# Projection of a deformable convolution: three f32r products from split values, or one fp32 product from a ring of twelve rows

## What is computed

```
yp = iy + ky + offset_y;  xp = ix + kx + offset_x          # per pixel, group and tap
val = gather(y0,x0)*(1-wy)*(1-wx) + gather(y0,x0+1)*(1-wy)*wx
    + gather(y0+1,x0)*wy*(1-wx)   + gather(y0+1,x0+1)*wy*wx
val = val * sigmoid(mask)
out = einsum('bhwkc,kcf->bhwf', val, dcn_w) + dcn_b        # the projection: 9*256 products per output
return x + relu(out) + fine_cal                            # all float32
```

## Time and profile before

| | before |
|---|---|
| median of three runs | 3750.42 us (3750.3 to 3751.57) |
| profiled execution | 3750.21 us, span 3748.5 us |
| busy TensorE / weight loads | 3383.5 us (90%) / 3082.7 us (82%) |
| busy VectorE / ScalarE / GpSimd | 2643.4 (71%) / 1636.7 (44%) / 1300.2 us (35%) |
| granted TensorE clock, mean | 0.956 of 2.4 GHz |
| costliest group | L1420, 8172 records, 1269.5 us |

### The profile page before, as it was taken

How to read it: one execution, slowest core, us unless ns; L and a number is a source line. 1 busy time by engine, 2 the same in 40 slices (tenths; PEclk the granted TensorE clock), 3 DMA queues, 4 the chain that set the end, 5 groups by cost and what they waited for, 6 DMA issues and landing times.

```text
span 3748.5 us, 103646 instructions
## 1 busy us (share of the span) xinstructions
PE 3383.5 (90%) x39276; PEld 3082.7 (82%) x39276; DVE 2643.4 (71%) x4029; ACT 1636.7 (44%) x3018; POOL 1300.2 (35%) x1358
## 2 busy tenths in 40 slices
PE   8979999999999947998888998998899898988998
PEld 7869999999999936888787887887788787877888
DVE  3446666666666548878876887886887887688882
ACT  0021211211221215656654665664666665566663
POOL 1000000000000025645645555554654655455451
PEclk9989999999999978999998999998999998999998
DMA  4232232222223221111112111112111112111110
GB/s 160 78 122 42 48 72 42 48 53 39 51 51 43 32 49 30 29 32 31 31 32 32 32 33 29 31 34 32 29 33 31 30 34 36 25 33 32 31 27 23
DMA packets 352248, 159.43 MB, mean 43 GB/s; under 512 B 228724, under 2 KB 346884, under 8 KB 351620
## 3 DMA queue, kind: packets, MB, share of 16 engines
q1 hardware_dynamic: 325456, 109.56, 17.4%
q10 hardware_dynamic: 21724, 26.37, 2.1%
q0 software_dynamic: 4608, 16.78, 1.2%
HBM read 104.60 MB, written 55.23 MB: 43 GB/s over the span
## 4 chain that ended last, share of the span: by engine, by line
PE 44%; issue 7%; ACT 6%; DVE 2%; POOL 2%; ACTq 1%; DMA 1%; SPq 1%; POOLq 0%; DVEq 0%
PE eb L1420 25%; PE tb L981 9%; PE vb L1003 9%; ACT wtT L986 4%; ACT ot L1025 1%; ACT res L1012 1%; DVE wt L975 1%; PE tb L911 1%; DMA win<-cpad 1%; ACTq L1316 1%; PE vb L1018 1%; ACT val L1289 1%; ACTq L882 0%; DVE val L1362 0%; SPq L1083 0%
## 5 line engine op out<-in xcount | busy, mean ns | idle before, releaser
L1420 PE MATMUL eb<-val,wd 128*128 128x256 f32 (+2 forms) x8172 | 1269.5, 300 | 9.5 <-POOL gate L1212 8.5
L1420 PEld LDWEIGHTS eb<-val,wd 128*128 128x128 f32 x8172 | 1080.6, 199 | 44.8 <-issue 35.4
L975 DVE TENSOR_TENSOR wt<-taps_all 128x576 f32<-128x576 f32 x1024 | 938.6, 984 | 52.5 <-PE tb L981 44.6
L981 PE MATMUL tb<-ident,wt 128*128 128x128 f32 x4608 | 715.9, 282 | 63.8 <-ACT wtT L986 45.3
L986 ACT COPY wtT<-tb 128x512 f32<-128x512 f32 x1152 | 651.8, 593 | 164.8 <-PE tb L981 126.0
L1362 DVE TENSOR_TENSOR val<-vb,val 128x432 fp32r<-128x432 f32 (+1 forms) x768 | 382.6, 552 | 411.0 <-ACT val L1289 409.2
L981 PEld LDWEIGHTS tb<-ident,wt 128*128 128x128 f32 x4608 | 504.7, 141 | 185.5 <-ACT wtT L986 103.6
L1289 ACT CAST val<-vb 128x432 fp32r<-128x432 f32 (+1 forms) x768 | 342.1, 524 | 706.4 <-PE vb L1003 706.2
L480 PE MATMUL conv<-fine,wf 128*108 128x256 f32 x4608 | 591.1, 289 | 7.6 <-DVE omT L751 7.6
L480 PEld LDWEIGHTS conv<-fine,wf 128*108 128x108 f32 x4608 | 570.5, 173 | 23.0 <-issue 23.0
L1003 PE MATMUL vb<-wtT,win 64*32 64x144 f32 x16384 | 350.2, 309 | 184.3 <-issue 93.3
(11 more groups left out here) (138 smaller groups left out, 3175.7 us busy)
## 6 DMA issues: line engine op xcount, KB each, us to landing
win<-cpad SPq DMA_DIRECT2D x304, 64.0 KB
om_s<-om_d SPq DMA_DIRECT2D x1152, 12.0 KB
chunk<-in_x SPq DMA_DIRECT2D x32, 512.0 KB, 5.9
xchunk<-in_x SPq DMA_DIRECT2D x32, 512.0 KB, 4.2
r_d<-r POOLq DMA_DIRECT2D x32, 512.0 KB, 3.2
rt<-r_d SPq DMA_DIRECT2D x63, 256.0 KB, 2.9
out<-ot ACTq DMA_DIRECT2D x63, 256.0 KB, 2.2
om_d<-omT SPq DMA_DIRECT2D x64, 216.0 KB
```

What stands on the lines that cost most here:

```text
L975: return nc.vector.tensor_tensor(wt[:, g * NK:(g + 1) * NK, WQ * u:WQ * (u + 1)].rearrange("p k (a b) -> p k a b", a=WIN), of_group(0).uns ...
L981: last = nc.tensor.transpose(tb[b][:, 128 * j:128 * j + 128], wt[:, 4 * i + j, :], ident[:])
L1420: done = nc.tensor.matmul(eb[fo][:, W * r0:W * r1], wd[wp][:, half, k, 128 * fo:128 * fo + 128], source[:, at:at + r1 - r0, cols], start=f ...
```

## The change

What it does:

- The projection is one fp32 product: 36 matmuls of 256 columns a strip, from one tensor val and one tensor wd. The split of the weights (`first_parts`, `second_parts`) and of the values (L1362) is gone; `keep_values` on ScalarE is the only copy.
- val has twelve rows a tap: each parity has two rows above and four of its own, so no read wraps. The two rows above are copies of the other parity's last two, made by SP with two DMAs a strip (`duplicate_rows`, taps 0 to 5).
- wt and wtT are two tiles each, one for each hx. A half is transposed in its slot, and sampled in the next slot, after batches 1 and 4; the projection is dealt out evenly, two matmuls behind each batch, half of a strip's in slot (t, 1) and half in (t+1, 0).
- Both fo lie in one bank eb, one bank for each parity; the result is turned into it too.
- Positions and coef are computed by VectorE (`locate`), distances stay on GpSimd. Groups are ordered so that window weights take six instructions of 768 elements instead of eight of 576.
- base_y and ctr_y hold one image's 16 strips. The general path is changed alike and isn't taken here.

The core of the diff:

```diff
-        wd = [sb(f"wd{q}", [128, CH, NK, C], f32r) for q in range(2)]
+        wd = sb("wd", [128, CH, NK, C])
...
-        wt = sb("wt", [128, GH * NK, 2 * WQ])
-        wtT = sb("wtT", [128, GH * NK, 128])
+        wt = [sb(f"wt{i}", [128, GH * NK, 2 * WQ]) for i in range(2)]
+        wtT = [sb(f"wtT{i}", [128, GH * NK, 128]) for i in range(2)]
...
-        VROWS, VCOLS = 9, W + 2
+        VROWS, VCOLS = 12, W + 2
+        val = sb("val", [128, CH, NK, VROWS, VCOLS])
...
+                def duplicate_rows(s, p):
...
+                    w(sp, "ready", opened)
+                    w(sp, "projected", read)
+                    dst, src = 6 * p, 6 * (1 - p) + 4
+                    for half in range(CH):
+                        sp.dma_start(val[:, half, 0:6, dst:dst + 2], val[:, half, 0:6, src:src + 2]
+                                     ).then_inc(sems["duplicated"], 16)
...
+                    if known(s - 2, 0, ST):
+                        load_rest(s - 2)
                     if known(s + 3, 0, ST):
                         w(sp, "batched", batch_no(s, 0, NT) + 1)
                         load_offsets(sp, s + 3, True, sems["om_loaded"])
...
+                    if known(s, 1, ST):
+                        duplicate_rows(s, p)
...
+                        side(t - 1, 1 - p, 1)
+                        open_strip(t - 1, 1 - p, crossing if p == 1 else None)
+                        measure(t + 1, 1 - p, 1)
+                        side(t, p, 0)
+                        add_rest(t - 2)
+                        measure(t + 2, p, 0)
...
+                def slot(t, p, hx):
...
+                    if hx == 1 and owed:
+                        w(act, "projected", t - 1)
+                        w(act, "turned", t - 2)
+                        for fo in range(CH):
+                            finish(fo, p, m).then_inc(sems["finished"], 1)
                     for i in range(NT):
...
+                            copy_batch("act", hx, i, bank_no(t, p, hx, i)).then_inc(sems["tb_out"], 1)
+                        if i == FIRST_RUNS_AT:
+                            keep_values(*half_before(t, p, hx), 0)
+                        if i == FIRST_RUNS_AT + 1:
+                            keep_values(*half_before(t, p, hx), 1)
+                        if i == THIRD_RUN_AT:
+                            keep_values(*half_before(t, p, hx), 2)
+                        if hx == 0 and i == 5:
+                            taps(t + 1, 1 - p, 0)
...
+                    if hx == 0:
+                        if known(t + 2, 0, ST):
+                            keep(t + 2, batch_no(t, 0, NT), bank_no(t, p, 0, NT))
+                        taps(t + 1, 1 - p, 1)
...
+                def slot(t, p, hx):
+                    products(*half_after(t, p, hx))
+                    if hx == 0:
+                        cap(t + 1, 1 - p, 0)
                     else:
+                        cap(t + 1, 1 - p, 1)
+                        locate(t + 2, p)
...
+                todo = [(dy, half, dx, fo) for dy in (2, 1, 0) for half in range(CH) for dx in range(3) for fo in range(CH)]
+                EACH = len(todo) // 2
+                SHARE = EACH // NT
...
+                        done = nc.tensor.matmul(eb[q][:, 256 * fo:256 * fo + rows], wd[:, half, k, 128 * fo:128 * fo + 128],
+                                                val[:, half, k, at:at + rows // W, dx:dx + W],
+                                                start=(n == 0), stop=(n == len(todo) - 1))
...
+                def slot(t, p, hx):
+                    n = 2 * t + hx
+                    target, q, first = (t - 1, 1 - p, 0) if hx else (t - 2, p, EACH)
                     for i in range(NT):
...
+                            transpose_batch(hx, i, bank_no(t, p, hx, i)).then_inc(sems["batched"], 1)
+                        if i == FIRST_RUNS_AT:
+                            first_runs(*half_before(t, p, hx))
+                        if i == THIRD_RUN_AT:
+                            third_run(*half_before(t, p, hx))
+                        if known(target, 0, ST + 1):
+                            if first == 0 and i == 0:
+                                w(pe, "ready", target + 1)
+                                w(pe, "ob_out", target - 1)
+                            last = project(target, q, range(first + SHARE * i, first + SHARE * (i + 1)))
...
+                        if hx == 1 and i == 6 and known(t - 2, 0, ST + 1):
+                            m = W if isinstance(t, int) and t - 2 == ST else 256
+                            w(pe, "summed", t - 1)
+                            turn_result(p, m).then_inc(sems["turned"], 1)
```

More of the change, by code:

```diff
@@ L1180, in side @@
                             else:
-                                dst, src = v[:, :, east, rows, W + 1], v[:, :, west, rows, W]
-                            g.tensor_copy(dst, src.bitcast(f32)).then_inc(sems["sides"], 1)
+                                dst, src = val[:, half, east, rows, W + 1], val[:, half, west, rows, W]
+                            last = g.tensor_copy(dst, src)
+                        last.then_inc(sems["sides"], 1)
                 def open_strip(s, p, crossing):
+                    above, under = slice(0, 3), slice(6, 9)
@@ L1186, in open_strip @@
+                    if known(s, 1, ST + 1):
+                        h(pool, "duplicated", 16 * CH * s)
                     if known(s, 0, ST):
-                        h(pool, "sides", 4 * (s + 1))
-                    if p == 1 and known(s, 0, ST):
-                        for v in val:
-                            g.tensor_copy(v[:, :, 3:6, 0], v[:, :, 3:6, 8].bitcast(f32)).then_inc(sems["below"], 1)
-                        h(pool, "below", s + 1)
-                    above, under = slice(0, 3), slice(6, 9)
@@ new lines, in keep_values @@
+                def keep_values(s, p, hx, v):
+                    if known(s, 0, ST):
+                        w(act, "sampled", 3 * (2 * s + hx) + v + 1)
+                        if hx == 0 and v == 0:
+                            w(act, "cleared", CLEARED)
+                            w(act, "ready", s)
+                            w(act, "projected", s - 1)
+                        x = 1 + 32 * hx + 12 * v
+                        for u in range(2):
+                            values = bank_of(u, v)
+                            nc.scalar.copy(val[:, u, :, 6 * p + 2:6 * p + 6, x:x + values.shape[3]], values).then_inc(sems["kept"], 1)
@@ L1395, in dve_fast @@
                     nc.vector.tensor_tensor(table[:, :, 2], table[:, :, 1], wide(at_start), ALU.subtract).then_inc(based, 1)
[L1396 to L1400 removed]
+                dve.wait_ge(based, BASED)
+                for s in range(2):
+                    locate(s, s)
+                for hx in range(2):
+                    cap(0, 0, hx)
@@ L1402, in pe_fast @@
+                products(0, 0, 0)
+                loop(dve, by_strip(slot))
             def pe_fast(pe):
-                todo = [(dy, half, dx, fo, part) for dy in range(3) for half in range(CH) for dx in range(3)
-                        for fo in range(CH) for part in range(3)]
+                todo = [(dy, half, dx, fo) for dy in (2, 1, 0) for half in range(CH) for dx in range(3) for fo in range(CH)]
+                EACH = len(todo) // 2
+                SHARE = EACH // NT
                 def project(s, q, items):
```

562 lines of the change are left out of this document (215 added, 347 removed).

## The result

The changed kernel takes 3543.6 us (median of four runs, 3531.2 to 3548.5) against 3751.0 (3750.3 to 3753.9) for the kernel before on the same chip: a ratio of 0.9441, with a 95% interval of 0.9415 to 0.9466. It is faster by 207 us; 102 were predicted. The time lies in the predicted range (3535 to 3770), 104 us under the predicted one. The profiled execution is the quickest of the four: 3531.2 for a span of 3529.5, 219 us under the 3748.5 of before.

The account below looks back on a forecast made before the run. TensorE was taken as nearest its limit, with gaps and lower clock. Strip 2's start 1459, 31 x 67.7 for pairs of strips, 3 x 16 for image starts, 40.5 for the end: span 3646, plus 1.9: 3648 us; range 3535 to 3770.

Parts of the forecast that it names:

- price of two strips: Sampling loop's regular pace: TensorE's work 60.0 us plus changes of matmul kind, loop turn, lower clock and waits, 67.7 us.
- rival of open weight loads: Projection: weight loads of fp32 records lie open at 256 columns; slower, 3795 us with a quarter open, 4220 wholly; chance 0.13.
- rival E: Projection: work grows by its passes, 237 us more, 3885 us; chance 0.03.
- Transposes: TensorE's batches of four transposes: 0.49 us a batch, 18 batches a strip, 8.8 us.
- Changes of kind: Sampling on TensorE: matmul kind changes four more times in two strips, estimated 0.6 us.
- ScalarE at hx=1: Head of hx=1: ScalarE's first wtT copy comes late for TensorE's batch 2, 0.9 us a strip, bounds 0 and 3.4.
- GpSimd's add: Add of rt behind side() on GpSimd ends late for TensorE: 0.3 us a strip, bounds 0 and 1.
- The turn: TensorE's loop turn stays as a gap of 2.9 us in two strips, with 1.7 lost to the lower clock after it.
- rival B: Whole loop: gaps nearly vanish and the denser array keeps full clock, 62.9 us for two strips, 3500 us; chance 0.13.
- Duplicates priced at 0: SP's copying of duplicated rows, 811 KB a strip: hidden, 0 us; uncovered it would be 9 us a strip.
- rival F: Duplicates land late and hold open_strip, the half projection and the taps by some 2 us a strip: 3776 us; chance 0.04.
- Rival C: Gaps change owner: part of ScalarE's 2.5 us of taps lies open each strip, 3741 us; reached in part, chance 0.17.

Follow-up runs that it names:

- the halved one: The changed kernel with half of the projection's matmuls left out (18 of 36 a strip): 3188.9 us, ratio 0.8516.
- the two kernels whose loops bring none: The changed kernel with half of the projection's matmuls left out, 3188.9 us; the kernel before with one fp32 product in the old order, 3692.0 us.

## Why the prediction was right in sign and short by half

Against the profiled span (3529.5 for 3646), by the parts of the sum:

- Start: strip 2's slot begins at 1466.7 (two batches before its first samples at 1468.5), forecast 1459: +8. TensorE waits 16.1 us for the first products at 1419.4. The positions of two strips took the 6 us on VectorE that I had allowed, but the second stood 6.9 us behind ScalarE's mask, and the first four caps took 6.9 us where I had 3.3.
- Tail: 41.6 for 40.5: +1. Image starts: waits of 13.1, 13.5 and 8.1 where I had 14, with half-rate samples behind them as forecast. The pairs of strips that hold them are 16.8, 17.0 and 9.8 us longer than the others, 44 in all for 48: -4.
- Pace: (3487.9 - 1466.7 - 44)/31 = 63.8 us for two strips, where the sum had 67.7. These 3.9 times 31 are 121 us, more than the whole error of 117.

So the step that failed is the price of two strips (67.7 us). Its large term, the projection at 15.7 us a strip, held; the transposes, the loop's turn with the clock behind it, and the waits for ScalarE and GpSimd were all priced too high:

- A record of 256 columns: 0.218 forecast, 0.2175 measured. The rival of open weight loads (D, 3795) is out, and the choice of L157 and L450 over L154 was right; what made L154's own records slow, no run tested. The Trainium skill (FP8 and Floating Point Precision, TensorE Precision Notes) gives true FP32 four passes through the array. The trace agrees: four passes of 256 columns at 2.4 GHz are 0.427 us by estimate, and the two records of a matmul take 0.435. The conclusion that work therefore grows (rival E, 3885) did not come true, because the old records stood at 117 and 124 ns.
- Transposes: priced at 0.49 a batch, measured 0.435 (1.305 less 0.87). Within a row a transpose starts 0.109 us before the next in both kernels, so that four are 0.435. The 0.055 more of the earlier trace rows lies where transposes and f32r matmuls of 0.124 follow each other, and between transposes and fp32 matmuls of 0.2175 it is gone. Whether that is by the longer record or by the type, no run separates. 36 x 0.055: 2.0 us. A price that I took from a row carried the cost of its old neighbour. This is the largest single miss.
- Changes of kind: 2407.20 to 2407.73 is 0.53 for 0.44, 2409.39 to 2410.36 is 0.97 for 0.87, 0.19 a sampling run and 1.56 for the eight in two strips, forecast 0.6: 1.0 the other way.
- ScalarE at hx=1: 14.7 us of waits in 60 strips. Start to start the delay is larger, at 2424.45 to 2425.88 it is 1.43 us for 0.97, and 0.46 a strip on average, where I had 0.9: 0.9 us less in two strips. GpSimd's add: no wait, 0.7 less.
- The ninth batch of hx=0, which comes while ScalarE makes tap weights ahead of its copies, and which my sum left out: it starts 1.06 us after the matmuls before it where others start 0.87 after, and takes 0.49, in every strip: 0.5 the other way. The view shows hardly any idle time there.
- The turn: 67 us of late starts over 31 pairs of strips, 2.2 each for 2.9: 0.7. Lower clock behind it: 85 us at the lower clock less 34 behind the image starts, 1.7 a turn, half of it lost: 0.85 for 1.7, so 0.85. Many turns now bring no fall: the clock fell 17 times from 1480 to 3400, 14 of them at turns, and 29 times in the kernel before.

Together 3.7 us less where 3.9 were found; the terms for the records and for the turning of offsets and result came out another 0.3 lower. It is rival B's direction, gaps that shrink and a clock that holds, gone about four fifths of its way (62.9). I gave B 0.13 and argued that the turn idles TensorE about as long as before; its gaps were 2.4 us in the mean (56.0 in 23) where they had been 3.3 (83.0 in 25).

Two of my choices hid this. The same sum made 72 for before where 70.0 was measured. I read that as "not short of work"; it could have been read as a sum too long by 2 us a pair, and subtracting that would have given 65.7 and 3586. It would have been closer partly by luck, since the largest miss, the transposes, was priced right for the kernel before. And I took the middle or upper value for five small waits at once (0.9, 0.35, 2.9, 1.7, 0.49), each defensible alone.

Duplicates priced at 0 were a miss the other way: where they stood they cost 44 to 50 us, 1.5 a turn, not by landing late (rival F: no wait on gate appears) but by lying just ahead of the turn. The forecast's turn of 2.9 us, taken from the kernel before, covered it by luck. Rival C (ScalarE's taps open, 3741) shows nowhere in the full kernel; in the halved one ScalarE does bound batches. VectorE's share was right in its result, busy 21 us a strip (1318 in 62) under the 27 allowed; the move was not needed: left on GpSimd the same work costs nothing in one place of its queue and 290 us in another, which the prediction did not weigh.

## What to carry to other kernels

Where the engine that bounds the kernel waits often and briefly, run the row-by-row sum for the kernel before first, and correct the forecast by what that sum is off. A start-to-start time belongs to a pair of neighbours: when an edit changes the neighbour, price the pair anew. Transfers that are hidden by length of cover may still have a wrong place: look at what runs just ahead of each loop turn, and at what stands behind a chain that begins with a wait. And count the instruction packets inside a loop: where they recur with every turn, a shorter body may be worth more than fewer turns.

## What the runs showed of the hardware

- A loop turn on TensorE cost 4.0 to 4.7 us with the clock behind it (60 to 70 us for 15 turns), and its bare gap went from a mean of 2.4 us (56.0 in 23) with a 792 KB copy under way just ahead of it to 1.7 (25.8 in 15) with the copy elsewhere. The Trainium skill (Runtime: NRT & Kernel Launch, Instruction fetch mechanics) says that a taken branch out of the present pages forces a fetch before execution goes on. The traces agree: bodies for which q8 brings some 140 KB of instructions a turn have the gap, TensorE goes on 1.7 us (median) after the last 16 KB packet landed, and the two kernels whose loops bring none have no gap.
- Within a row a 128x128 fp32 transpose starts 0.109 us before the next, in both kernels. Four of them and two f32r matmuls of 256 columns recur after 0.74 us, 0.055 more than their parts; four of them and four fp32 records after 1.305, the sum of theirs.
- VectorE's position steps of 288 elements took 0.30 to 0.71 us (means of a step), GpSimd's 1.0 to 2.5 for the same (medians, with the positions back on GpSimd); GpSimd's 72-element adds 0.9 to 1.0 us, VectorE's 0.24 and 0.49.
- The sixteen window loads kept TensorE waiting 9.4 to 11 us at an image's start even when they were issued in half the time.
